# A two-layer transformer on one core: the first layer's attentions write their outputs by feature, their division moves into the stage that reads them

## The chip, the core and the metric

The kernel runs on one core of a Trainium2 chip. The core has TensorE (PE in the profile; its weight loads are listed as PEld), VectorE (DVE), ScalarE (ACT), GpSimd (POOL) and SyncE (SP), whose queue issues most transfers. Each engine works through its own instructions in order and waits at semaphores. The metric is the device time of one execution in microseconds, median over the runs shown. About 0.2% (some 7 us) is what a measurement of this kernel can tell from no change.

## What is computed

Batch 8, 512 tokens, 320 features, 20 heads of 16, a context of 64 tokens; two layers of self-attention, cross-attention and a gated feed-forward part. Only the first layer's attentions change; it is plain floating point:

```
def _attn(x, ctx, wq, wk, wv, wo, bo, heads):
    q = (x @ wq).reshape(b, n, heads, dh).transpose(0, 2, 1, 3)
    k = (ctx @ wk).reshape(b, j, heads, dh).transpose(0, 2, 1, 3)
    v = (ctx @ wv).reshape(b, j, heads, dh).transpose(0, 2, 1, 3)
    sim = jnp.einsum('bhid,bhjd->bhij', q, k) * scale
    a = jax.nn.softmax(sim, axis=-1)
    out = jnp.einsum('bhij,bhjd->bhid', a, v)
    out = out.transpose(0, 2, 1, 3).reshape(b, n, heads * dh)
    return out @ wo + bo
h1 = _ln(x, n1_g, n1_b)
x = _attn(h1, h1, q1, k1, v1, o1_w, o1_b, heads) + x
h2 = _ln(x, n2_g, n2_b)
x = _attn(h2, context, q2, k2, v2, o2_w, o2_b, heads) + x
h3 = _ln(x, n3_g, n3_b)
proj = h3 @ ff_w1 + ff_b1
a, g = jnp.split(proj, 2, axis=-1)
x = a * jax.nn.gelu(g, approximate=False) @ ff_w2 + ff_b2 + x
```

The second layer has the same shape, with operands rounded to 8 bits in its attentions, and does not change.

## The kernel before

**Stages.** `transformer` runs one stage after another; at the end of a stage all engines meet. In the first layer: `dense_phase` "qkv" (to 207 us of the trace), `self_attention` (207 to 699), `dense_phase` "q" (to 850), `cross_attention` (853 to 1028), `dense_phase` "ff" (to 1550). Attention results go from stage to stage through DRAM. A group of attention is 4 heads of one sample: 5 groups a sample, 40 in all.

**Self-attention.** A group is 8 units (`for j in range(UNITS)`). In unit j TensorE does, for the group two ahead, two score tiles `nat` [128 queries x 512 keys] (`natural`, L1250), whose row maxima VectorE reduces one tile at a time (L1391); then the transposed scores of its own group, `sT` (`transposed`, L1259), on which ScalarE takes the exponential into `probs` (L1325); then, for the group before, `products` (L1277). One call of `products` is 4 matmuls in fp32, which the profile counts as 8 instructions; a group has 8 calls. There are three `nat` banks, and tile t waits until the reduction of tile t-3 is done:

```
wait(pe, "a_nat_free", 16 * n + t - 2)
```

The maxima are split by GpSimd into three bf16 parts, turned on TensorE (`turn_shift`), copied and sent into the query stack as extra rows. Each output column block has 32 rows, 16 of the head's values and one of the exponentials' sum. `turn_output` (L1287) turns the result back to token order, ScalarE copies it twice (L1318, L1334), VectorE takes the reciprocal of the sums (L1385), GpSimd multiplies (L1352), SP stores 128 KB as rows of 256 bytes.

**Cross-attention.** The same with 64 keys, so that a group is one unit: `natural` for three groups ahead (L2017), `transposed` (L2026), `turn_shift` (L2034), `turn_output` (L2052), `products` (L2044). ScalarE: exponential, copy of the shift, two transfers of it (L2092), copy of the output (L2098). VectorE: two reductions (L2156), reciprocal (L2132), product (L2134). Meanwhile GpSimd splits weights of the coming stage (`loader.turn`, one job a group in the first eleven groups) and adds the output bias to the residual (`early.add`, L306, the first 32 groups).

**Dense stages.** `loop` walks the samples with a hand-written list of steps (`body`), several samples in flight. Here `oT` turns the attention output to feature order on TensorE (12 transposes a sample, L848), ScalarE rounds it (`oT_hi`, L949), VectorE subtracts (`oT_lo`, L1012), `oproj` multiplies by the output weights. The second layer's dense stages have `by_feature=True`: their input lies by feature already and `oT` needs no TensorE work.

## Time and profile before

| what | us |
|---|---|
| median of 3 runs | 3343.64 (3338.16 to 3344.39) |
| the profiled execution, its own time | 3342.7 |
| its span in the trace | 3341.0 |
| self-attention, one group in steady state | 11.57 |
| cross-attention, one group in steady state | 3.48 |
| feed-forward, one sample: first layer / second layer | 61.55 / 60.15 |
| "q" stage, one sample: first layer / second layer | 15.45 / 13.86 |

TensorE is busy 88% of the span, VectorE 65%, ScalarE 57%, GpSimd 24%. TensorE's granted clock is 0.84 on average and 1.00 inside the long stages. The periods in the table are differences between starts of the same operation: 39 of the copies L1318 for self-attention, the exponentials L2084 for cross-attention, the operations L804 (one a sample) for the dense stages. Busy times of TensorE overlap their neighbours' pipelines; starts tell more than durations there.

### The profile page before, as it was taken

The page shows a single profiled execution, that of the slowest core. Times are in us where ns is not written, and L with a number is a line of the kernel's source. Part 1 is how long each engine was busy: PE and PEld are TensorE (multiplying, and loading weights), DVE is VectorE, ACT ScalarE, POOL GpSimd, SP SyncE. Part 2 cuts the span into 40 slices and gives each one's busy share as a digit, 9 for nine tenths or more (in the row PEclk, how much of TensorE's full clock was granted, in tenths as well). Part 3 has the DMA queues.
Part 4 walks back from the last instruction along what each step waited for, and adds up shares of the span by engine and source line. Part 5 has one row for each costly group of instructions (what it writes and reads, how often), then busy time and mean ns, then how long its engine had stood idle before and what let it go on. Part 6 is the DMA issues. An engine that isn't in the chain of part 4 may idle for free. (4 is left out here: it accounts for less than half of the span.)

```text
span 3341.0 us, 47964 instructions
## 1 busy us (share of the span) xinstructions
PE 2936.9 (88%) x15594; PEld 1775.7 (53%) x15594; DVE 2157.7 (65%) x3834; ACT 1892.4 (57%) x3214; POOL 805.5 (24%) x1149
## 2 busy tenths in 40 slices
PE   6989999978696999998959999879978577899999
PEld 5754444457455888886731111111126342788888
DVE  5668888837453444444649999968868685444443
ACT  4328888844353232233549999989975355333322
POOL 2021221114640000000027888200003471200000
PEclk9969999989798999998975555555559898899999
DMA  8663333336762000001567557266723213010000
GB/s 228 211 166 101 106 107 103 90 80 158 165 176 46 10 10 19 9 0 38 152 173 163 128 137 164 32 90 83 97 56 96 79 45 92 26 36 18 25 17 16
DMA packets 358243, 296.57 MB, mean 89 GB/s; under 512 B 175602, under 2 KB 281914, under 8 KB 358058
## 3 DMA queue, kind: packets, MB, share of 16 engines
q1 hardware_dynamic: 347994, 273.93, 34.0%
q0 software_dynamic: 7280, 18.07, 2.1%
q10 hardware_dynamic: 2784, 2.29, 0.4%
q8 instruction: 94, 1.54, 0.2%
q14 instruction: 91, 0.75, 0.1%
HBM read 177.53 MB, written 114.52 MB: 87 GB/s over the span
## 5 line engine op out<-in xcount | busy, mean ns | idle before, releaser
L1591 PE MATMUL nat<-k_stack,q_stack 48*128 48x512 bf16 x640 | 381.0, 605 | 71.5 <-DMA k_stack<-k1w 31.1
L1391 DVE TENSOR_REDUCE neg_max<-nat 128x1 f32<-128x512 f32 x640 | 400.7, 682 | 61.3 <-PE nat L1250 61.2
L1625 DVE TENSOR_REDUCE m_all<-nat 128x1 f32<-128x512 f32 x640 | 423.3, 691 | 18.1 <-PE nat L1591 17.8
L804 POOL TENSOR_TENSOR rstd<-var_eps,neghalf 128x4 f32<-128x4 f32 x48 | 51.9, 1081 | 1588.0 <-DVE var_eps L1028 1588.0
L1645 ACT ACTIVATE nat<-nat,m_all 128x512 f32<-128x512 f32 x640 | 427.7, 2130 | 3.0 <-DVE m_all L1625 2.9
L1645 ACT ACTIVATION_READ_ACCUMULATOR nat<-nat,m_all 128x1 f32 x640 | 403.6, 1674 | 0.0
L1054 DVE SCALAR_TENSOR_TENSOR ff<-outp,bias,gel 128x512 f32<-128x512 f32 x160 | 120.1, 751 | 417.6 <-PE outp L326 417.6
L1325 ACT ACTIVATE probs<-sT 128x1024 f32<-128x1024 f32 x320 | 328.0, 1027 | 93.1 <-PE sT L1259 85.5
L968 ACT ACTIVATE gel<-outp,bias 128x512 f32<-128x512 f32 x160 | 110.0, 688 | 351.6 <-PE outp L326 351.6
L1839 ACT ACTIVATE exps<-sT 128x1024 f32<-128x1024 f32 x320 | 293.4, 1573 | 10.5 <-PE sT L1788 10.5
L972 ACT CAST ff_hi<-ff 128x512 fp32r<-128x512 f32 x160 | 99.2, 620 | 312.3 <-DVE ff L1054 312.3
L1591 PEld LDWEIGHTS nat<-k_stack,q_stack 48*128 48x128 bf16 x640 | 64.1, 102 | 387.9 <-ACT nat L1645 350.8
L1876 DVE TENSOR_SCALAR probs<-exps 128x1024 bf16<-128x1024 f32 x320 | 218.3, 692 | 67.8 <-ACT exps L1839 67.8
L1788 PE MATMUL sT<-q_stack,k_stack 51*128 51x512 bf16 x640 | 194.2, 604 | 34.6 <-DMA q_stack<-shift_rows 12.2
L1250 PE MATMUL nat<-k_stack,q_stack 48*128 48x512 f32 x640 | 200.8, 524 | 20.1 <-DMA k_stack<-k_hi 11.7
L1277 PE MATMUL o_ps<-probs,v_stack 128*32 128x256 f32 x2560 | 199.8, 394 | 1.1 <-issue 1.1
L1057 DVE TENSOR_TENSOR ff_lo<-ff,ff_hi 128x512 fp32r<-128x512 f32 x160 | 122.1, 763 | 109.7 <-ACT ff_hi L972 109.7
L1048 DVE TENSOR_TENSOR hT_lo<-h,hT_hi 128x512 fp32r<-128x512 f32 x144 | 111.6, 780 | 106.0 <-ACT hT_hi L963 105.7
L1250 PEld LDWEIGHTS nat<-k_stack,q_stack 48*128 48x128 f32 x640 | 80.0, 193 | 163.6 <-DVE neg_max L1391 129.2
L1259 PE MATMUL sT<-q_stack,k_stack 51*128 51x512 f32 x640 | 157.7, 430 | 0.5 <-ACT probs L1325 0.2
L1788 PEld LDWEIGHTS sT<-q_stack,k_stack 51*128 51x128 bf16 x640 | 34.0, 102 | 184.0 <-ACT exps L1839 165.7
L326 PE MATMUL outp<-hT_hi,Wff_hi 128*128 128x512 f32 x320 | 125.9, 393 | 4.6 <-DVE hT_lo L1048 4.6
(561 smaller groups left out, 7163.3 us busy)
## 6 DMA issues: line engine op xcount, KB each, us to landing
v<-vpad SPq DMA_DIRECT2D x64, 320.0 KB, 2.8
q_stack<-q_part SPq DMA_DIRECT2D x90, 160.0 KB, 5.8
k_stack<-k1w SPq DMA_DIRECT2D x90, 160.0 KB, 10.5
q_stack<-q_hi SPq DMA_DIRECT2D x160, 64.0 KB, 2.5
v_stack<-v SPq DMA_DIRECT2D x40, 256.0 KB, 3.2
q_stack<-q_hi SPq DMA_DIRECT2D x80, 128.0 KB, 2.8
raw<-v SPq DMA_DIRECT2D x16, 640.0 KB, 14.9
k_stack<-k_hi SPq DMA_DIRECT2D x158, 64.0 KB, 2.2
```

The source lines that it names most:

```text
L326: mm = pe.matmul(out, stay, move, start=(n == 0), stop=(n == len(terms) - 1))
L1250: pe.matmul(nat[(16 * n + t) % 3][:, :], q_stack[half, n % RING, pr, qt * P:(qt + 1) * P], k_stack[half, n % RING, pr, :], start=True, sto ...
L1259: mm = pe.matmul(sT[use % 2][:, ab, :], k_stack[half, n % RING, pr, kt * P:(kt + 1) * P], q_stack[half, n % RING, pr, :], start=True, stop ...
L1277: mm = pe.matmul(o_ps[VCOL * h:VCOL * h + VCOL, tok], v_stack[:, n % 2, kt, VCOL * h:VCOL * h + VCOL], probs[:, n % 2, h, kt, tok], start= ...
L1325: act.activation(probs[:, n % 2, 2 * pr:2 * pr + 2, kt, :], sT[use % 2][:, :, :], ACT.Exp, scale=DH ** -0.5).then_inc(s["a_turn_free"], 1)
L1391: dve.tensor_reduce(neg_max[:, n % 2, qt, 2 * pr + ab:2 * pr + ab + 1], nat[(16 * (n + 2) + t) % 3][:, :], AX.X, ALU.max, negate=True).the ...
L1591: pe.matmul(bank[i % NAT][:, :], q_stack[half, slot, g, pr, qt * P:(qt + 1) * P], k_stack[half, slot, g, pr, :], start=True, stop=True).th ...
L1625: dve.tensor_reduce(k.m_all[:, column(i // TILES, i % TILES)], bank[i % NAT][:, :], AX.X, ALU.max, negate=True).then_inc(s["e_max_ready"], 1)
L1645: act.activation(b[:, :], b[:, :], ACT.Exp, bias=k.m_all[:, col], accum_out=k.s_all[:, col]).then_inc(s["a_nat_free"], 1)
L1788: mm = pe.matmul(sT[u % TURNS][:, ab, :], k_stack[half, slot, g, pr, kt * P:(kt + 1) * P], q_stack[half, slot, g, pr, :], start=True, stop ...
L1839: act.activation(exps[:, u % EXPS], sT[u % TURNS][:, :, :], ACT.Exp).then_inc(s["a_turn_free"], 1)
L1876: dve.tensor_scalar(probs[:, u % KEPT], exps[:, u % EXPS], ROUND, -ROUND, ALU.add, ALU.add).then_inc(s["e_rounded"], 1)
```

## The change

Both first-layer attentions store the untransposed, undivided product tile (`o_sb`, 128 rows of 2 KB, 256 KB a group), two buffers in turn. Once a sample, the 20 rows of sums are read back from DRAM into an 80 x 128 tile (`load_sums`), VectorE takes one reciprocal (`invert`), and the shares are stored (`store_shares`); in self-attention GpSimd first splits them into a high and a low part (`split_shares`). The dense stage that follows loads the output by feature and multiplies it on VectorE (step `scale`): in "q" against a PSUM tile that one TensorE matmul with a 0/1 matrix `spread` makes from the 40 rows of shares, in "ff" against an SBUF tile that eight transfers fill by broadcasting. `oT` loses its transposes; the ff stage issues 8 loads a sample instead of 5.

In self-attention `turn_output`, its two copies' second, the per-group reciprocal and product go, and the 8 calls of `products` stand two by two in units 1, 3, 5 and 7. In cross-attention `turn_output` goes, VectorE instead of ScalarE copies the output, the query loads are issued for two groups at a time, the shift goes in one transfer, GpSimd does a loader job every fourth group (4 jobs instead of 10) and the bias in the last 32 groups; the other 6 jobs of `ff_w2` are done by GpSimd at the start of the ff stage, as in the second layer.

TensorE in self-attention, from the start of unit 1 to the start of unit 5. In the names nat_172 to nat_174 are the three score banks, sT_175 and sT_176 the two transposed ones. Before:

```order
L1250 MATMUL nat_172<-k_stack,q_stack 128x512
L1250 MATMUL nat_173<-k_stack,q_stack 128x512
L1259 MATMUL sT_175<-q_stack,k_stack 128x512 x2
L1267 MATMUL sT_176<-identb,parts 32x128 x4
L1277 MATMUL o_ps<-probs,v_stack 32x256 x4
L1250 MATMUL nat_174<-k_stack,q_stack 128x512
L1250 MATMUL nat_172<-k_stack,q_stack 128x512
L1259 MATMUL sT_175<-q_stack,k_stack 128x512 x2
L1287 MATMUL sT_176<-ident,o_sb 128x128 x4
L1277 MATMUL o_ps<-probs,v_stack 32x256 x4
L1250 MATMUL nat_173<-k_stack,q_stack 128x512
L1250 MATMUL nat_174<-k_stack,q_stack 128x512
```

Now:

```order
L1315 MATMUL nat_171<-k_stack,q_stack 128x512
L1315 MATMUL nat_172<-k_stack,q_stack 128x512
L1324 MATMUL sT_174<-q_stack,k_stack 128x512 x2
L1332 MATMUL sT_175<-identb,parts 32x128 x4
L1342 MATMUL o_ps<-probs,v_stack 32x256 x8
L1315 MATMUL nat_173<-k_stack,q_stack 128x512
L1315 MATMUL nat_171<-k_stack,q_stack 128x512
L1324 MATMUL sT_174<-q_stack,k_stack 128x512 x2
L1315 MATMUL nat_172<-k_stack,q_stack 128x512
L1315 MATMUL nat_173<-k_stack,q_stack 128x512
L1324 MATMUL sT_175<-q_stack,k_stack 128x512 x2
L1342 MATMUL o_ps<-probs,v_stack 32x256 x8
```

The output's transposes (L1287) and the single calls of products (x4) of units 2 and 3 are gone from here; unit 1 and unit 3 end with two calls (x8), unit 2 with none.

TensorE in cross-attention, one group. Before:

```order
L2017 MATMUL nat_246<-k_stack,q_stack 128x128 x4
L2017 MATMUL nat_247<-k_stack,q_stack 128x128 x4
L2026 MATMUL sT_248<-q_stack,k_stack 128x512 x2
L2034 MATMUL sT_249<-identb,parts 32x128 x4
L2052 MATMUL o_ps_250<-ident,o_sb 128x128 x4
L2044 MATMUL o_ps_251<-probs,v_stack 64x512 x2
```

Now:

```order
L2086 MATMUL nat_245<-k_stack,q_stack 128x128 x4
L2086 MATMUL nat_246<-k_stack,q_stack 128x128 x4
L2095 MATMUL sT_247<-q_stack,k_stack 128x512 x2
L2103 MATMUL sT_248<-identb,parts 32x128 x4
L2113 MATMUL o_ps_250<-probs,v_stack 64x512 x2
```

The four transposes L2052 between the turning of the shift and the products are gone.

VectorE in the "q" stage, the second half of a round, from the normalised rows z to the last addition of oproj; the next round follows with the statistics of x_resid. The banks oT hold the turned output before, and the spread shares now. Before:

```order
L1034 TENSOR_SCALAR z<-x_resid,mv,rstd 128x320 x4
L1016 TENSOR_TENSOR x_resid<-x_resid,oproj_224 128x320
L1048 TENSOR_TENSOR hT_lo<-h_214,hT_hi 128x512 x2
L1016 TENSOR_TENSOR x_resid<-x_resid,oproj_225 128x320
L1048 TENSOR_TENSOR hT_lo<-h_214,hT_hi 128x512
L1016 TENSOR_TENSOR x_resid<-x_resid,oproj_224 128x320
L1016 TENSOR_TENSOR x_resid<-x_resid,oproj_225 128x320
```

Now:

```order
L1092 TENSOR_SCALAR z<-x_resid,mv,rstd 128x320 x4
L1074 TENSOR_TENSOR x_resid<-x_resid,oproj_225 128x320
L1106 TENSOR_TENSOR hT_lo<-h_215,hT_hi 128x512 x2
L1074 TENSOR_TENSOR x_resid<-x_resid,oproj_226 128x320
L1106 TENSOR_TENSOR hT_lo<-h_215,hT_hi 128x512
L1064 TENSOR_TENSOR attn_T<-attn_T,oT_229 128x512
L1064 TENSOR_TENSOR attn_T<-attn_T,oT_230 128x512
L1074 TENSOR_TENSOR x_resid<-x_resid,oproj_225 128x320
L1064 TENSOR_TENSOR attn_T<-attn_T,oT_229 128x512
L1074 TENSOR_TENSOR x_resid<-x_resid,oproj_226 128x320
```

Three multiplications attn_T (L1064) have come in behind the last hT_lo, before and between the last two additions of oproj, and the differences oT_lo now read their result. The diff, cut to its core:

```diff
 dense_phase:
+        scale = [("scale", m) for m in range(3)] if recips is not None else []
-            between = [[("tail", 0)], oT[0:2], oT[2:], oproj[0:2], oproj[2:], [("stats", 0)], [("norm", 0)],
+            between = [[("tail", 0), *scale], oT[0:2], oT[2:], oproj[0:2], oproj[2:], [("stats", 0)], [("norm", 0)],
...
-                    zT[0], zT[1], oproj[1], zT[2], oproj[2], oproj[3]]
+                    zT[0], zT[1], oproj[1], zT[2], *scale[0:2], oproj[2], *scale[2:], oproj[3]]
...
+                        heads = rows(attn_in, b * (QUADS * P), QUADS * P).rearrange("(h c) t -> h c t", c=VCOL)[:, 0:DH, :]
+                        loads = [(attn, heads)]
...
+                        for tile, src in loads:
+                            for c in range(2):
+                                sp.dma_start(tile[:, c, :], src[8 * c:8 * c + 8]).then_inc(s["attn_in_loaded"], 16)
...
+                        pe.matmul(bank_of(st, r)[:, :], spread[:, m * P:(m + 1) * P], shares[:, :], start=True, stop=True
+                                  ).then_inc(s[turned[st][0] + "_full"], 1)
...
+                        dve.tensor_tensor(attn[:, m, :], attn[:, m, :], share, ALU.mult).then_inc(s[done], 1)
 self_attention:
+                    for r in range(2):
+                        wait(sp, f"a_o_stored{r}", 16 * ((QUADS * (b + 1) - r + 1) // 2))
+                    sums_of = rows(out, b * (QUADS * P), QUADS * P).rearrange("(h c) t -> h c t", c=VCOL)[:, DH, :]
+                    sp.dma_start(sums, sums_of.rearrange("h (x t) -> h x t", t=P)
...
-                def turn_output(n):
...
-                PRODUCTS = {1: (0,), 2: (1,), 3: (2,), 4: (3, 4), 5: (5,), 6: (6,), 7: (7,)}
+                PRODUCTS = {1: (0, 1), 3: (2, 3), 5: (4, 5), 7: (6, 7)}
...
-                        act.copy(o_sb[:, :], o_ps[:, :]).then_inc(s["a_o_copied"], 1)
+                        wait(act, f"a_o_stored{n % 2}", 16 * (n // 2 - 1))
+                        act.copy(o_sb[:, n % 2, :], o_ps[:, :]).then_inc(s["a_o_copied"], 1)
...
-                            act.copy(o_turned[:, n % 2, :], output_bank(n - 2)).then_inc(s["a_turn_free"], 1)
...
+                    pool.tensor_copy(share_hi, shares).then_inc(s["a_share_split"], 1)
...
+                    dve.reciprocal(shares, sums).then_inc(s["a_recip"], 1)
 cross_attention:
-                    for n in range(LOOK, RING):
-                        load_q(n)
+                for pair in range(2, PAIRS):
+                    load_q(pair)
...
-                        for pr in range(2):
-                            act.dma_start(words(q_stack[QROWS:ROWS, (n + 2) % RING, pr, :]),
+                        act.dma_start(words(q_stack[QROWS:ROWS, (n + 2) % RING, :, :]), words(shift_sb[0:12, n % 2, :])
...
-                    loader.turn(pool, n)
-                    if n < BATCH * TT:
-                        early.add(pool, n)
+                    if n % 4 == 3 and n // 4 <= len(loader.jobs):
+                        loader.turn(pool, n // 4)
+                    if n >= NQ - BATCH * TT:
+                        early.add(pool, n - (NQ - BATCH * TT))
...
+                    dve.tensor_copy(o_sb[:, n % 2, :], o_ps[n % 2][:, :]).then_inc(s["x_o_copied"], 1)
```

## Rows read from the trace of the kernel before

**Rows 1.** Busy time by engine in stretches (us, instructions), clock, DMA share, GB/s:

```profile
753.10:799.46 46.36, 40.64 (x240) 33.66 (x240) 36.86 (x79) 23.66 (x40) 20.68 (x28) 1.00 0.67 168
858.00:915.00 57.00, 44.52 (x218) 27.86 (x218) 21.71 (x40) 20.43 (x28) 45.86 (x97) 0.71 0.81 179
915.00:1015.00 100.00, 99.25 (x628) 57.80 (x626) 54.43 (x113) 56.26 (x86) 43.88 (x138) 1.00 0.62 159
940.00:980.00 40.00, 40.00 (x257) 23.59 (x256) 22.65 (x46) 22.61 (x35) 19.55 (x56) 1.00 0.70 178
1165.04:1411.23 246.19, 246.19 (x1346) 219.19 (x1345) 106.42 (x204) 74.29 (x116) 15.83 (x8) 1.00 0.06 13
3018.29:3258.88 240.59, 240.59 (x1296) 214.11 (x1296) 106.45 (x204) 74.72 (x116) 15.82 (x8) 1.00 0.07 21
```

**Rows 2.** TensorE's timeline in self-attention: start, us, operation, idle before it:

```profile
449.91 0.54 PE L1250 MATMUL nat<-k_stack,q_stack 48*128 48x512 f32 x2
...
451.26 0.49 PE L1250 MATMUL nat<-k_stack,q_stack 48*128 48x512 f32 x1 [0.21 <-DVE neg_max L1391]
...
453.65 0.63 PE L1287 MATMUL sT<-ident,o_sb 128*128 128x128 f32 x4
...
456.01 0.54 PE L1250 MATMUL nat<-k_stack,q_stack 48*128 48x512 f32 x2
...
456.72 1.07 PE L1277 MATMUL o_ps<-probs,v_stack 128*32 128x256 f32 x16
457.72 0.50 PE L1250 MATMUL nat<-k_stack,q_stack 48*128 48x512 f32 x2
...
458.38 0.64 PE L1277 MATMUL o_ps<-probs,v_stack 128*32 128x256 f32 x8
458.95 0.55 PE L1250 MATMUL nat<-k_stack,q_stack 48*128 48x512 f32 x2
```

**Rows 3.** VectorE's timeline in the same stretch:

```profile
458.26 3.80 DVE L1391 TENSOR_REDUCE neg_max<-nat 128x1 f32<-128x512 f32 x6 [0.42 <-PE nat L1250]
```

**Rows 4.** Timeline of one group of cross-attention:

```profile
942.75 1.38 ACTq L2092 DMA_DIRECT2D q_stack<-shift_sb  x2
...
943.05 1.11 PE L2017 MATMUL nat<-k_stack,q_stack 96*128 96x128 f32 x8
...
944.22 0.59 ACT L2098 COPY o_sb<-o_ps 128x512 f32<-128x512 f32 x1 [1.51 <-issue]
...
944.94 0.66 PE L2052 MATMUL o_ps<-ident,o_sb 128*128 128x128 f32 x4
...
945.52 1.08 PE L2044 MATMUL o_ps<-probs,v_stack 128*64 128x512 f32 x4
...
946.53 0.33 PE L2017 MATMUL nat<-k_stack,q_stack 96*128 96x128 f32 x1
```

**Rows 5.** Who waited for whom, start of cross-attention: us, times, longest:

```profile
PEld sT L2034 <- POOL parts L2119: 13.3, 8, 3.2
```

**Rows 6.** Groups of instructions: VectorE's, busy us and mean ns:

```profile
L1391 DVE TENSOR_REDUCE neg_max<-nat 128x1 f32<-128x512 f32 x640 | 400.7, 682 | 61.3 <-PE nat L1250 61.2
...
L2132 DVE RECIPROCAL recip<-o_ps 128x16 f32<-128x16 f32 x40 | 10.3, 258 | 45.4 <-PE o_ps L2052 27.8 <-DMA cross_out<-o_nat 17.6
...
L2541 DVE RECIPROCAL red<-red 128x1 f32<-128x1 f32 x1 | 0.2, 164 | 0.0
```

**Rows 7.** Timeline from cross-attention's end into the feed-forward stage:

```profile
1023.21 1.08 PE L2044 MATMUL o_ps<-probs,v_stack 128*64 128x512 f32 x4
...
1028.87 2.09 SPq L691 DMA_DIRECT2D attn_nat<-cross_out  x4
...
1039.56 0.60 PE L326 MATMUL misc<-q_hi,oT_hi 128*128 128x320 f32 x1 [1.49 <-DVE oT_lo L1012]
```

**Rows 8.** Transfer rate in 40 one-us slices of cross-attention:

```profile
GB/s 83 196 255 151 135 102 233 227 197 277 245 215 208 105 244 177 99 48 26 99 221 199 155 153 209 270 201 244 262 259 206 99 264 183 97 99 155 251 170 87
```

**Rows 9.** Transfer issues of cross-attention: count, KB each, median us to landing:

```profile
cross_out<-o_nat SPq DMA_DIRECT2D x40, 128.0 KB, 2.6
```

290 lines of the change are left out of this document (167 added, 123 removed).

## The prediction

> **What bounds the kernel now.** I read the busy time by stage first, then the timelines of one group. The averages hide that each stage has its own limit, and that only the six stages between 207 us and the end of the first feed-forward stage can move.
>
> Self-attention is TensorE and VectorE in turns. A pair of score tiles and a pair of transposed tiles each take about 0.33 us (the two matmuls of a pair run side by side): in unit 5 `nat` starts at 456.01 and the products at 456.72. Eight product instructions last 0.57 to the next `nat` (458.38 to 458.95), sixteen last 1.00 (456.72 to 457.72) [rows 2]. The only stall inside the group is at 451.26, where the second tile of unit 1 waits 0.21 us for a reduction, 1.35 us after unit 0's first tile went out at 449.91 [rows 2]. VectorE is not full either: in the same stretch it waits 0.42 us for TensorE, then does six reductions in 3.80 us [rows 3]. So neither is the bound; the three score banks couple them.
>
> Cross-attention is TensorE back to back in steady state (99.25 of 100 us), with the 16 DMA engines at 0.62 on average and 0.70 in the densest 40 us [rows 1]. One group there: score tiles at 943.05, output turned at 944.94, products at 945.52, next score tiles at 946.53 [rows 4]. Its first stretch is different: TensorE is busy 44.52 of 57 us at a granted clock of 0.71, GpSimd 45.86 [rows 1], and turning the shift waits 8 times, 13.3 us in all, for GpSimd's `parts` [rows 5].
>
> **Self-attention, per group.** The change takes TensorE's output turn away: 454.20 - 453.65 = 0.55 us [rows 2]. It also moves the products into the odd units, and that costs the banks. A reduction lasts 0.68 us [rows 6] and the next starts (3.80 - 0.68) / 5 = 0.62 after it [rows 3]; a tile's reduction can start when its matmul is over, 0.54 us after the tile (the length of the pair at 449.91) [rows 2]. So a bank is free some 0.54 + 0.68 + 0.06 = 1.28 us after its tile starts, 0.06 being my estimate for the two signals. The row measured 1.35 [rows 2], and I keep that for the upper end. Tile t waits for tile t-3, that is, the second tile of a unit waits for the first of the unit before. An even unit now has 0.66 us of work and no products behind it; the next unit's second tile starts 1.28 us after the even unit's first, then follow 0.33 + 0.32 until the products and 1.00 of products: 2.93 us for a pair of units. The pair with the shift's turn gets 0.17 more. The group: 3.10 + 3 x 2.93 = 11.89, against 11.57. This is +0.32 x 37 groups = +11.8. ScalarE, with one copy less, does not set this. The last groups have no score tiles for a later group; there the turn is pure gain, 2 x 0.55, and the drain behind the last product loses a copy and the division, which I estimate at 0.8: -1.9. **Self-attention +9.9.** Bounds: lag 1.35 gives 12.17 a group, so +0.60 x 37 - 1.9 = +20.3. Below, TensorE's own work is 8 x 0.66 + 4 x 1.00 + 0.33 = 9.6 us and the reductions' 16 x 0.62 = 9.9, which no order of three banks reaches.
>
> **The "q" stage.** Its head now waits for a chain behind the last output: store (2.6 us to landing [rows 9], as before), the sums' load back (no row; like the store, 2.6), the reciprocal, GpSimd's split, the shares' store, the loads, one matmul, three multiplications. The reciprocal of 128 columns: 16 take 258 ns and 1 takes 164 [rows 6], 6.3 ns a column, so 164 + 127 x 6.3 = 0.96 us. The split is two small GpSimd copies, 0.9 by estimate. What goes is the old turn, copy, reciprocal and product. Part of the chain runs beside the stage's start (weights, statistics). I take +2.0 for the head and +1.8 for the second sample's load, which is issued behind it: +3.8, between 1 and 8. In the rounds TensorE saves 12 transposes, four of which last 0.55 [rows 2], so some 1.6 us less one to three matmuls of 0.2, say 1.2; VectorE gets 3 multiplications of about 0.6 us at the end of the round, on the path to the next statistics. The stretch shows TensorE busy 40.64 of 46.36 us and VectorE 36.86 [rows 1], so neither covers the other: +0.3 a round, from -0.3 to +1.8, times 7: +2.0. The second layer's 13.86 a round has neither cost. **"q" +5.8.**
>
> **Cross-attention.** The output's turn leaves TensorE: 945.52 - 944.94 = 0.58 us a group [rows 4], 3.48 - 0.58 = 2.90. ScalarE loses its output copy of 0.59 and one of two transfer issues (1.38 for both) [rows 4], so it isn't the bound afterwards; VectorE exchanges reciprocal and product for one copy. I take 2.95, a little waiting: -0.53 x 31 = -16.4. In the first groups GpSimd's loader jobs go from every group to every fourth: the 13.3 us of waits [rows 5] go, -13.3. The bias, moved to the last 32 groups, is GpSimd work beside a mostly idle engine (43.88 of 100 [rows 1]). The first pair of query loads has to land whole, +1.7. **Cross-attention -28.**
>
> The stores grow from 128 to 256 KB a group [rows 9]. At 178 GB/s for a share of 0.70 [rows 1] the extra 128 KB are 0.74 us x 0.70 = 0.52 of share-time, on top of 0.70 x 3.48 = 2.44; over 2.95 us the share would be 1.00. That is too much for comfort, yet slices of 1 us reach 277 GB/s [rows 8], and in them the same kinds of rows move; 750 KB in 2.95 us are 254 GB/s. The densest stretch lasts only part of the stage; at the mean share, 0.62, it is (2.16 + 0.50) / 2.95 = 0.90.
>
> The new rows are 2 KB long, the old 256 bytes. The Trainium skill ("DMA: Bandwidth & Descriptors", Why small descriptors are slow) counts 256/32 + 3 = 11 cycles for a descriptor of 256 bytes; by that rule the new store would cost 2 x 67 / 88 = 1.52 times the old one, not twice, so half of the 0.52. No row here decides it, and the sum stands without it.
>
> **The "ff" stage.** A round loses the 12 transposes and comes to look like the second layer's: 246.19 / 4 = 61.55 against 240.59 / 4 = 60.15 us [rows 1]. Six rounds in steady state: -8.4. Its head: before, the first load is issued 5.66 us after the last products (1023.21, 1028.87), the first `oproj` matmul comes at 1039.56 [rows 7]. Now the store, the sums' load (2.6), the reciprocal (0.96) and the shares' store (2.6) come first, +6.2; gone are turn, reciprocal and product (about 1.5) and the transposes and their copies (1.7): +3.0, and 0.6 for more loads a sample. Six `ff_w2` jobs on GpSimd run beside the first rounds, where it is busy 15.83 of 246 us [rows 1]: nothing. **"ff" -4.8**, between -8 and +1.
>
> The second layer's code is the same: 0. **Sum:** +9.9 + 5.8 - 28 - 4.8 = -17.1 on the profiled execution's 3342.7; it lies 0.9 under the median, which gives 3326.5.
>
> **The rivals.**
>
> *Self-attention gains.* If the pairs of units overlapped better than the bank rule says, say at 10.7 a group, between 9.9 and 11.89, self-attention would give -0.87 x 37 - 1.9 = -34, and the time 3326.5 - 44 = 3282. For it: TensorE loses work. Against: the stall at 451.26 already shows the rule with products in the unit before it, and even units without products leave 0.62 us bare [rows 2].
>
> The Trainium skill ("TensorEngine Tiling (Array Packing)", PSUM Bottleneck) says that tiling speeds up TensorE but not the reading of PSUM. The idle row at 451.26 agrees: a tile waits for its reduction, so by that rule less TensorE work shows in the time only where the reductions keep up.
>
> *Cross-attention gains less.* If the DMA engines carry 0.92 of the denser stretch, a group takes 2.96 / 0.92 = 3.2 and the stage gives -8.7 for the period, -9 for the head: -18; with a lag of 1.30 to 1.31 self-attention costs 12.0 a group, +14, and "q" +7. Sum -1.8: 3342. For it: the transfers' share of 1.00 above. Against: rates of 277 GB/s.
>
> *The slower side: the DMA engines bound cross-attention.* The highest share that a long stretch shows is 0.81 [rows 1]. If that is what they carry, a group takes 2.96 / 0.81 = 3.65, longer than 3.48; it decides from a share-time of 2.8 a group on. The period costs +5 (0.17 x 31), the gain at the head goes into the same transfers, and the whole is +9.9 + 5.8 + 5 - 4.8 = +16: 3359. For it: at 0.81 GpSimd was the one who was late, so higher was never asked for. Against: exactly that reason, and [rows 8].
>
> *The change doesn't do what it says:* the order shows the turns gone in both stages, so I give it nothing.
>
> **How the numbers follow.** My forecast 0.60, self-attention gains 0.09, cross-attention gains less 0.20, the slower side 0.11. The forecast's own unknowns (self-attention +10 to +20, "q" +2 to +12, cross-attention -34 to -22, "ff" -8 to +1) spread it over some 3300 to 3344. The range leaves out the fast rival and the slow one: 3298 to 3347. A measurement of this kernel tells 0.2%, 6.7 us, from no change. Faster than 3337: 0.56 of the forecast, all of the 0.09 and 0.05 of the third, 0.70; slower than 3350: 0.11 and a little, 0.12; between: 0.18.
>
> **What would show it.** In the changed kernel a self-attention group of 11.9 us (12.2 with the longer lag, under 11.3 if I am wrong), VectorE idle before `neg_max` by TensorE four times a group, and TensorE idle 0.6 us by VectorE before the second tile of units 1, 3, 5 and 7. In cross-attention 2.95 us a group with TensorE unbroken, or 3.2 to 3.65 with waits on transfers of `q_stack`, and the waits for `parts` gone. "q" rounds of 15.7 us, and "ff" rounds of 60.2. The first `oproj` of "ff" some 19 us behind the last products instead of 16.4. A self-attention group at or under 11.57 would break the largest uncertain term; a cross-attention group above 3.3 would break the largest gain.

## The result

The changed kernel takes 3412.96 us (median of 4 runs, 3406.32 to 3429.98), the kernel before 3343.68: a ratio of 1.0219, with a 95% interval of 1.018 to 1.0258. It is slower by 69 us where 17 us less were forecast. The profiled execution took 3406.3 us with a span of 3404.4.

Where it went, by the start of the same operation in both traces (first reduction of self-attention; last `products`; the operation `rstd`, one a sample; first exponential of cross-attention; and so on), with what the prediction had for the stretch:

| stretch | before | after | change | forecast |
|---|---|---|---|---|
| self-attention | 487.6 | 499.1 | +11.5 | +9.9 |
| to the first `rstd` of "q" | 26.9 | 41.3 | +14.4 | +3.8 |
| the seven rounds of "q" | 107.4 | 148.4 | +41.0 | +2.0 |
| to the first exponential of cross-attention | 42.2 | 46.1 | +3.9 | +1.7 |
| cross-attention | 151.3 | 140.5 | -10.8 | -29.7 |
| to the first `rstd` of "ff" | 26.5 | 37.7 | +11.2 | +3.6 |
| "ff" from there | 504.2 | 495.0 | -9.2 | -8.4 |
| second layer | 1786.6 | 1788.7 | +2.1 | 0 |

The rows sum to 64.1 us; the two spans (3341.0 and 3404.4) are 63.4 apart, since the stretch before self-attention is 0.8 shorter; the medians are 69 apart. Here are busy times by stretch (columns as in [rows 1]): the last six rounds of "q", cross-attention, a part of it, and four rounds of "ff", in the changed kernel.

```profile
768.70:896.50 127.80, 100.76 (x429) 77.81 (x428) 87.40 (x172) 46.88 (x77) 43.76 (x55) 0.81 0.38 119
942.00:1080.00 138.00, 127.63 (x670) 68.37 (x668) 74.99 (x116) 57.37 (x77) 70.66 (x202) 0.87 0.80 196
1010.00:1025.00 15.00, 15.00 (x52) 7.63 (x51) 6.64 (x10) 4.44 (x6) 5.07 (x15) 0.50 0.97 214
1233.10:1473.90 240.80, 240.80 (x1298) 214.22 (x1297) 113.50 (x216) 74.80 (x116) 15.80 (x8) 1.00 0.08 26
```

"q" is what stands out: TensorE is busy 100.76 of 127.80 us at a granted clock of 0.81, where [rows 1] had 40.64 of 46.36 at 1.00. Cross-attention runs at a DMA share of 0.80 and a clock of 0.87, and has a stretch of 15 us entirely at the lower clock (0.50, that is 1.2 GHz). The "ff" rounds are the 60.2 us that were forecast (240.80 / 4).

Where an experiment below has no interval, it is one run, and its stages say more than its time. The four runs of the changed kernel lie 24 us apart, and traces in which the code of a stage is the same give 499.1 to 501.1 us for self-attention (nine traces), 148.4 to 150.6 for the rounds of "q" (eight), but 137.8 to 144.8 for cross-attention (seven).

The timeline of one round of "q", from the last use of `attn_T` to the next sample's cast (start, us, operation, idle before it):

```profile
816.23 0.93 DVE L1070 TENSOR_TENSOR oT_lo<-attn_T,oT_hi 128x512 fp32r<-128x512 f32 x1
...
817.35 0.34 SPq L692 DMA_DIRECT2D shares<-self_shares  x1
...
817.88 1.61 SPq L696 DMA_DIRECT2D attn_T<-self_out  x2
...
819.69 1.22 SPq L698 DMA_DIRECT2D attn_T<-self_out  x2
...
827.14 1.22 PE L887 MATMUL oT<-shares,spread 40*128 40x512 f32 x2 [3.92 <-DMA attn_T<-self_out]
827.97 1.28 DVE L1064 TENSOR_TENSOR attn_T<-attn_T,oT 128x512 f32<-128x512 f32 x2 [2.05 <-PE oT L887]
...
831.55 0.69 DVE L1064 TENSOR_TENSOR attn_T<-attn_T,oT 128x512 f32<-128x512 f32 x1
...
833.98 1.14 ACT L990 CAST oT_hi<-attn_T 128x512 fp32r<-128x512 f32 x2 [8.78 <-PE oproj L326]
```

There is one tile `attn_T`. Its last reader is the third `oT_lo`, which ends at 817.16. The next sample's loads are issued at 817.35, 817.88 and 819.69, and land at 827.1. TensorE, due for the `scale` step of the same round some 6 us after the first issue, waits 3.92 us for them. In TensorE's order the matmuls with `spread` stand in front of the last two `oproj`, so these wait too. VectorE's three multiplications end at 832.24, but the cast that follows starts only at 833.98: what released it was the last `oproj`, which reads the tile that the cast overwrites. Then comes `oT_lo` again, and the circle closes, through TensorE's order as much as through the multiplications. The waits of the stretch 768 to 882 say it in two lines (us, times, longest):

```profile
ACT oT_hi L990 <- PE oproj L326: 43.8, 5, 9.1
...
PE oT L887 <- DMA attn_T<-self_out: 20.1, 5, 4.3
```

In the kernel before the same circle had slack:

```profile
769.24 0.66 PE L848 MATMUL oT<-ident,attn_nat 128*128 128x128 f32 x4 [1.32 <-DVE oT_lo L1012]
...
770.08 3.01 SPq L691 DMA_DIRECT2D attn_nat<-self_out  x4
...
780.54 1.03 PE L848 MATMUL oT<-ident,attn_nat 128*128 128x128 f32 x8
```

The tile was free as soon as TensorE had turned it, the loads were issued from 770.08 and had landed by 777.9, and the next turn was due only at 780.54: 10.5 us after the first issue, with 2.7 to spare.

Self-attention, TensorE, one group of the changed kernel:

```profile
412.08 0.49 PE L1315 MATMUL nat<-k_stack,q_stack 48*128 48x512 f32 x1 [0.30 <-DVE neg_max L1443]
...
413.73 0.50 PE L1315 MATMUL nat<-k_stack,q_stack 48*128 48x512 f32 x2
...
414.31 0.40 PE L1315 MATMUL nat<-k_stack,q_stack 48*128 48x512 f32 x1
415.01 0.50 PE L1315 MATMUL nat<-k_stack,q_stack 48*128 48x512 f32 x1 [0.31 <-DVE neg_max L1443]
...
417.96 0.50 PE L1315 MATMUL nat<-k_stack,q_stack 48*128 48x512 f32 x1 [0.32 <-DVE neg_max L1443]
...
420.97 0.50 PE L1315 MATMUL nat<-k_stack,q_stack 48*128 48x512 f32 x1 [0.37 <-DVE neg_max L1443]
```

The second tile of units 1, 3, 5 and 7 waits 0.30 to 0.37 us of TensorE's idle time for a reduction: 412.08, 415.01, 417.96, 420.97 are 2.93, 2.95 and 3.01 apart. That is the picture forecast, beside the one stall of 0.21 in [rows 2]; the idle time itself is about half of the 0.6 us that the prediction named as its sign.

### The profile page after: what moved, and what is told of

It is laid out like the page before. It is cut to its first block and busy times, and to the rows that moved or that the text cites. A ratio compares the mean times of both kernels' runs of the same rounds, so it can differ in the third digit from the quotient of the medians.

```text
span 3404.4 us, 46635 instructions
## 1 busy us (share of the span) xinstructions
PE 2913.3 (86%) x15106; PEld 1779.3 (52%) x15106; DVE 2199.1 (65%) x3820; ACT 1862.2 (55%) x3134; POOL 789.3 (23%) x1125
## 5 line engine op out<-in xcount | busy, mean ns | idle before, releaser
L1680 DVE TENSOR_REDUCE m_all<-nat 128x1 f32<-128x512 f32 x640 | 423.9, 690 | 18.3 <-PE nat L1646 18.0
L1380 ACT ACTIVATE probs<-sT 128x1024 f32<-128x1024 f32 x320 | 326.8, 1025 | 116.3 <-PE sT L1324 114.2
L1315 PE MATMUL nat<-k_stack,q_stack 48*128 48x512 f32 x640 | 236.9, 497 | 59.8 <-DVE neg_max L1443 47.3
L1843 PE MATMUL sT<-q_stack,k_stack 51*128 51x512 bf16 x640 | 194.1, 604 | 33.5 <-DMA q_stack<-shift_rows 10.9
L1315 PEld LDWEIGHTS nat<-k_stack,q_stack 48*128 48x128 f32 x640 | 96.7, 192 | 206.6 <-DVE neg_max L1443 142.6
L1324 PE MATMUL sT<-q_stack,k_stack 51*128 51x512 f32 x640 | 186.9, 433 | 1.1 <-ACT probs L1380 1.1
L1342 PE MATMUL o_ps<-probs,v_stack 128*32 128x256 f32 x2560 | 174.0, 386 | 0.9 <-issue 0.9
L990 ACT CAST oT_hi<-attn_T 128x512 fp32r<-128x512 f32 x96 | 56.0, 618 | 148.7 <-PE oproj L326 82.4
## 6 DMA issues: line engine op xcount, KB each, us to landing
k_stack<-k1w SPq DMA_DIRECT2D x90, 160.0 KB, 10.5
```

What stands on the lines that cost most here:

```text
L1315: pe.matmul(nat[(16 * n + t) % 3][:, :], q_stack[half, n % RING, pr, qt * P:(qt + 1) * P], k_stack[half, n % RING, pr, :], start=True, sto ...
L1324: mm = pe.matmul(sT[use % 2][:, ab, :], k_stack[half, n % RING, pr, kt * P:(kt + 1) * P], q_stack[half, n % RING, pr, :], start=True, stop ...
L1342: mm = pe.matmul(o_ps[VCOL * h:VCOL * h + VCOL, tok], v_stack[:, n % 2, kt, VCOL * h:VCOL * h + VCOL], probs[:, n % 2, h, kt, tok], start= ...
L1380: act.activation(probs[:, n % 2, 2 * pr:2 * pr + 2, kt, :], sT[use % 2][:, :, :], ACT.Exp, scale=DH ** -0.5).then_inc(s["a_turn_free"], 1)
L1680: dve.tensor_reduce(k.m_all[:, column(i // TILES, i % TILES)], bank[i % NAT][:, :], AX.X, ALU.max, negate=True).then_inc(s["e_max_ready"], 1)
L1843: mm = pe.matmul(sT[u % TURNS][:, ab, :], k_stack[half, slot, g, pr, kt * P:(kt + 1) * P], q_stack[half, slot, g, pr, :], start=True, stop ...
```

## Experiments: the q stage

In the diffs `...` stands for lines left out, and most semaphore updates (`then_inc`) and counts are left out too.

**Two tiles** (a_two_tiles). `attn_T` and `shares` twice in "q", used in turn, on the changed kernel:

```diff
-            attn = sb("attn_T", [P, 3, TOK])
+            attns = [sb("attn_T", [P, 3, TOK]) for _ in range(tiles)]
...
-                        sp.wait_ge(s["oT_split"], at["oT_split"] + split_b * 3 + 3)
+                        sp.wait_ge(s["oT_split"], at["oT_split"] + (split_b + 1 - tiles) * 3 + 3)
```

> The changed kernel, with two tiles attn_T and two tiles of shares in the q stage, used in turn, so that a sample's load starts two splits (oT_lo) earlier. Theory (the load of the single tile attn_T, 9 to 10 us from first issue to landing, is exposed in each round because its old content is read until oT_lo and the scale step of the same round needs the new): q rounds fall from 22 us to 15.4 to 16.5, the granted clock there rises from 0.8 to about 1.0, the time falls by some 45 us. Rival 1 (the added work, three multiplications and three matmuls, sets the round): rounds stay at 20 us or more. Rival 2 (the added transfers fill the DMA engines): rounds stay above 18 with a higher DMA share.

Measured 3370.38 us, 42.6 less than the changed kernel's median (35.9 in the span). The stretch of the rounds:

```profile
741.70:858.20 116.50, 93.90 (x485) 73.48 (x486) 97.44 (x198) 52.91 (x86) 47.02 (x58) 0.97 0.44 135
```

The seven rounds take 116.5 us instead of 148.4, at a clock of 0.97. That is just above the 15.4 to 16.5 us a round of the theory (16.6 on average). In the middle of the stage a round is 17.2 us, against 15.45 before; the 1.75 us are near the 3 x 0.6 of the multiplications, which are probably the second, smaller cost: no run takes them out. The head is 34.0 us instead of 41.3.

**The same work later** (a_scale_late). `scale` at the front of its own round, one tile:

```diff
-                ahead["scale"] = 3
+                ahead["scale"] = 2
-            body = [("stats", 0), *oT[0:2], items[0], oT[2], ...
-                    zT[0], zT[1], oproj[1], zT[2], *scale[0:2], oproj[2], *scale[2:], oproj[3]]
+            body = [("stats", 0), *scale[0:2], *oT[0:2], items[0], *scale[2:], oT[2], ...
+                    zT[0], zT[1], oproj[1], zT[2], oproj[2], oproj[3]]
```

> The changed kernel with one tile attn_T as it is, but with the scale step of a sample moved from the second half of the round before to the front of its own round, ahead of its oT steps (two samples ahead instead of three). The work is the same, the load gets about half a round more. Theory (the load is exposed): rounds of 16.5 to 18.5 us, so 25 to 40 us less in all, since the multiplications now stand in a chain with the casts. Rival (the work sets the round): 21 us or more.

3378.65 us; rounds of 18.3 on average, and the clock back at 0.97. The place of the step alone, with the same work and one tile, gives 20.4 us of the 41 back.

**A load that reaches more DMA engines** (a_compact). The share of the engines during the first load of the changed kernel's "q" stage, and the rate, in 40 slices of 0.35 us from 713 to 727 us:

```profile
DMA  0000004400327125555545423224432100000000
GB/s 0 0 0 0 23 15 103 101 16 0 146 88 59 41 70 187 205 199 193 217 193 159 95 77 94 76 100 101 95 66 31 1 0 0 0 0 0 0 0 0
```

The share is 5 tenths at some 200 GB/s while the transfers of 8 heads run and 2 to 4 tenths at 76 to 101 GB/s while those of 4 heads run. So I packed the values in DRAM when self-attention stores them:

```diff
-                        sp.dma_start(rows(out, (n - 2) * P, P), o_sb[:, n % 2, :])
+                        for h in range(4):
+                            sp.dma_start(rows(out, (n - 2) * 64 + DH * h, DH), o_sb[VCOL * h:VCOL * h + DH, n % 2, :])
+                        sp.dma_start(rows(out, NQ * 64 + (n - 2) * 4, 4), o_sb[DH:P:VCOL, n % 2, :])
...
+                            sp.dma_start(tile[:, 0:2, :], src[0:2 * P].rearrange("(c p) t -> p c t", p=P))
```

> The changed kernel, in which self-attention stores the 4 x 16 rows of values next to each other in DRAM (four transfers of 32 KB) and the 4 rows of sums apart (8 KB), so that the q stage loads a sample with one transfer of 512 KB over 128 partitions and two of 64 KB instead of two of 8 heads x 16 rows and two of 4 heads x 16 rows. One tile attn_T, products as in the changed kernel. Theory (the transfers by head reach only as many DMA engines as they have heads: the rate is 200 GB/s in the first part and 100 in the second, a share of 0.5 and 0.25): the load falls from 8.9 to 9.8 us to 5 to 7 us from first issue to the first matmul that waits for it, the q rounds from 21.2 us to 17 to 19 us, the stage's head by some 8 us, the time by 25 to 40 us. Rival (the load is slow because it stands behind the stores and the weight loads): under 8 us in all.

3376.76 us. The head and two of the loads, in slices of 1.05 us from 698 to 740:

```profile
GB/s 18 89 216 70 23 0 0 0 0 0 76 49 77 9 63 63 8 39 0 0 24 62 129 345 322 33 1 0 0 0 0 6 123 371 326 2 0 0 0 0
```

The loads now run at 322 to 371 GB/s, and the rounds take 116.4 us, the same as with two tiles: either cure is enough for the exposed load, and what remains (9 us over the 107.4 before) lies in the round's own work, by size the multiplications. Both together gave no more in the rounds (below). But self-attention grew by 5.4 us: single groups took up to 13.1 us.

## Experiments: self-attention

**The old spread of the products, on the changed kernel** (a_old_products):

```diff
-                PRODUCTS = {1: (0, 1), 3: (2, 3), 5: (4, 5), 7: (6, 7)}
+                PRODUCTS = {1: (0,), 2: (1,), 3: (2,), 4: (3, 4), 5: (5,), 6: (6,), 7: (7,)}
```

> The changed kernel with the calls of products spread over the units of a self-attention group as in the kernel before (one each in units 1, 2, 3, 5, 6, 7, two in unit 4). Theory (three score banks: the second tile of a unit waits for the reduction of the first tile of the unit before, so a unit without products leaves TensorE idle): the group falls from 12.04 us to 10.9 to 11.2, and the time by 32 to 44 us. Rival (reductions or exponentials set the group, or the copies): the group stays within 0.2 us of 12.04.

3371.77 us, a group 10.94 us instead of 12.07 (self-attention 462.0 instead of 499.1 us). TensorE's timeline keeps one stall, in unit 1:

```profile
340.52 0.50 PE L1315 MATMUL nat<-k_stack,q_stack 48*128 48x512 f32 x1 [0.22 <-DVE neg_max L1443]
...
342.03 0.49 PE L1315 MATMUL nat<-k_stack,q_stack 48*128 48x512 f32 x2
...
343.36 0.49 PE L1315 MATMUL nat<-k_stack,q_stack 48*128 48x512 f32 x2
...
344.60 0.54 PE L1315 MATMUL nat<-k_stack,q_stack 48*128 48x512 f32 x2
```

Units follow each other 1.24 to 1.33 us apart, about the 1.28 that a bank needs, and none of these waits. So taking the turn away is worth 0.63 us a group, and grouping the products costs 1.13.

**The grouping alone, on the kernel before** (b_grouped), the same edit the other way:

> The kernel before with the products of a self-attention group in four pairs (units 1, 3, 5, 7), nothing else. Theory (bank rule): the even units get bare time, of which the output's turn in unit 2 fills one; the group goes from 11.57 to 12.0 to 12.2 us, about as long as in the changed kernel, and the time rises by 17 to 24 us. Rival (the turn costs its 0.55 us wherever it stands, grouping costs 1.0): 12.6 us a group, plus 40 us. Rival 2 (grouping costs nothing; what made the changed group long is another part of it): 11.57.

3370.77 us, 12.38 a group: between the two theories. Units 2 and 3:

```profile
341.39 0.50 PE L1250 MATMUL nat<-k_stack,q_stack 48*128 48x512 f32 x2
...
342.06 0.65 PE L1287 MATMUL sT<-ident,o_sb 128*128 128x128 f32 x4
342.65 0.52 PE L1250 MATMUL nat<-k_stack,q_stack 48*128 48x512 f32 x2
343.25 0.50 PE L1259 MATMUL sT<-q_stack,k_stack 51*128 51x512 f32 x2
```

The turn at 342.06 does fill the bare time of unit 2, but it takes one of the two `sT` banks: the transposed scores of unit 3 start 0.60 us after their score tiles instead of the 0.34 of unit 2. Of the 0.31 us by which this group is longer than the changed kernel's, most lies there. That the bank is what they wait for is read from the order of the uses, not tried.

## Experiments: cross-attention

**Fewer bytes by fewer rows** (x_small_store). Only the 17 rows a head that are read later:

```diff
-                        sp.dma_start(rows(out, (n - 2) * P, P), o_sb[:, n % 2, :])
+                        for h in range(4):
+                            sp.dma_start(rows(out, (n - 2) * P + VCOL * h, DH + 1),
+                                         o_sb[VCOL * h:VCOL * h + DH + 1, n % 2, :])
```

> The changed kernel, in which cross-attention stores only the 4 x 17 rows of each output tile that are read later (16 of values and the sum for each head), in four transfers, 136 KB instead of 256 KB a group. Theory (the DMA engines bound cross-attention in its dense stretches: share 0.93 to 0.97, 741 KB a group at 216 GB/s are 3.4 us): with some 620 KB a group the mean distance of exponentials falls from 3.56 us to 2.9 to 3.15 and cross-attention takes 15 to 25 us less. Rival (the loads of two groups at once delay the small transfers of the shift, whatever the stores are): the waits of sT for q_stack<-shift_sb stay above 10 us in all and the stage changes by under 6 us. Rival 2 (the number of transfers counts, not their bytes): slower than before the edit.

3546.79 us: 134 us more than the changed kernel's median, for 120 KB less a group. Cross-attention took 260.6 us. The rate in slices of 1 us:

```profile
GB/s 25 27 25 65 203 297 215 209 103 75 64 47 25 17 58 154 190 27 43 28 16 98 320 207 213 27 27 25 61 47 25 27 61 320 215 233 41 27 41 41
```

Between the query loads the rate sits at 25 to 27 GB/s. Of the three outcomes written down, the second rival (the number of transfers counts) had the sign right, but nothing of this size; the rate looked like one DMA engine carrying a whole transfer, and the next run tells the two apart.

**Four transfers of 32 rows, the same bytes as the one** (x_four32):

```diff
-                        sp.dma_start(rows(out, (n - 2) * P, P), o_sb[:, n % 2, :])
+                        for h in range(4):
+                            sp.dma_start(rows(out, (n - 2) * P + VCOL * h, VCOL),
+                                         o_sb[VCOL * h:VCOL * h + VCOL, n % 2, :])
```

> The changed kernel with cross-attention's store as four transfers of 32 whole rows (64 KB each), the same bytes as one of 128 rows. In x_small_store four transfers of 17 rows ran at 25 to 27 GB/s, a sixteenth of the highest rate. Theory (17 rows can't be divided among several DMA engines and one carries them all; 32 can): cross-attention within 10 us of the 140 of the changed kernel. Rival (four issues a group in place of one are what cost 120 us): 200 us or more.

3436.31 us, cross-attention 161.0 us: neither theory's number. Against 17 rows the stage is 100 us shorter, so the 17 rows are what cost most; but four transfers in place of one still cost it 20.5 us. Where they lie:

```profile
DVE m_all L2194 <- DMA m_all<-cross_out: 19.5, 7, 4.7
...
PE nat L2088 <- DVE neg_max L2214: 14.6, 4, 5.2
```

VectorE waits 19.5 us for the sums to come back from DRAM (9.1 in the changed kernel), its reductions stand behind that wait, and TensorE waits 14.6 us for these, which it never did in the changed kernel. SyncE meanwhile waited 20.5 us for VectorE's copies (48.6 in the changed kernel), so its queue was fuller but not full. Whether the three issues more delay the sums, or stores in four parts land later, isn't told apart.

**Five transfers, 136 KB** (x_compact): the packing of the q stage's experiment, in cross-attention and "ff".

> The changed kernel with the same packing of the output in cross-attention: five transfers, 136 KB a group instead of one of 256 KB, and the ff stage loads a sample's values with one transfer over 128 partitions and two over 64. Theory 1 (bytes bound cross-attention): mean distance of exponentials from 3.56 us to 3.1 to 3.2, the stage 12 to 18 us shorter; the head of ff 3 to 6 us shorter, since half of its loads is now quick. Theory 2 (the stretches at the lower clock and what starts them bound it): the stage within 6 us. Rival (SyncE's queue becomes the bound, five issues a group instead of one are some 1.5 us more): the stage is longer, the stores start late.

3432.92 us, cross-attention 167.8 us. The bytes fell by 120 KB a group and the stage grew, so bytes don't bound it. SyncE's issues add up to 137.8 us of the 164.9 between first and last exponential (71.0 of 138.8 in the changed kernel), as the rival with the queue has it; but VectorE's wait for the sums is as long as with four transfers (19.7 us), and what delays them is again not told apart. "ff" got no faster head (37.4), since its loads of the shares still go by head.

**Twice the bytes** (x_double_store): each tile stored a second time.

```diff
+                        for copy in range(2):
+                            sp.dma_start(rows(out, (copy * NQ + n - 2) * P, P), o_sb[:, n % 2, :])
```

> The changed kernel, in which cross-attention stores each output tile twice, the second time to a place that nobody reads: 256 KB and one issue a group more. x_four32 had three issues more and no bytes and took 20.5 us more, so one issue is worth some 7 us. Theory (bytes bound the stage, 741 KB a group at 216 GB/s): 1000 KB a group are 4.6 us, the stage goes from 140 us to 180 or more. Rival (SyncE's queue, the chain of the sums or the bursts bound it): 145 to 155 us.

3422.67 us, cross-attention 153.3 us. The stretch 930 to 1080:

```profile
930.00:1080.00 150.00, 130.99 (x640) 73.57 (x640) 72.21 (x111) 50.73 (x69) 66.42 (x196) 0.77 0.95 239
```

The engines carry 239 GB/s at a share of 0.95. The changed kernel's 196 at 0.80 was no limit of the stage: 10 MB more cost 12.8 us, under a third of what the theory of the bytes needs. For short stretches its engines were as full (0.97 from 1010 to 1025), so that a small transfer can be late there is not excluded.

**Query loads for one group at a time** (x_single_q):

```diff
-                def load_q(pair):
+                def load_q(n):
...
-                    if exists(n - 1) and exists(n - 1 + RING) and n % 2 == 0:
+                    if exists(n - 1) and exists(n - 1 + RING):
```

> The changed kernel, in which cross-attention's query loads are issued for one group at a time again, as in the kernel before (three of 128 KB instead of three of 256 KB for two), with 8 semaphores instead of 4; the bytes are the same. Theory (bytes bound the stage): no more than 5 us less or more. Rival (bursts of 768 KB delay the shift's transfer behind them): the waits of sT for q_stack<-shift_sb fall from 15 us to under 5, the stage takes 10 to 20 us less.

3402.21 us. The first exponential comes 5.6 us sooner; the stage is 2.5 us shorter, which is inside the 7 us of its spread and not the 10 to 20 of the rival. TensorE's weight loads of `sT` waited for the shift's transfer 12 times, 13.9 us in all, from 942 to 1083 in the changed kernel; now:

```profile
DVE m_all L2191 <- DMA m_all<-cross_out: 16.7, 7, 4.6
...
PEld sT L2094 <- DMA q_stack<-shift_sb: 4.4, 4, 1.8
```

So the bursts did delay that transfer (from issue to landing 4.6 us at the median in the changed kernel, 3.1 now). What the stage kept is the wait of VectorE for the sums (12.2 us of the 16.7 lie before the last products at 1076.7; its reductions stand behind it) and, behind its start, 31 us at the lower clock, as many as the changed kernel has.

**The sums later** (x_lazy_sums):

```diff
-                    if exists(n - 3) and (n - 3) % PER == PER - 1:
-                        load_sums((n - 3) // PER)
+                    for last in range(NQ - 1, -1, -PER):
+                        if n == min(last + 5, NQ + 2):
+                            load_sums(last // PER)
...
-                    if exists(n - 4) and (n - 4) % PER == PER - 1:
-                        invert((n - 4) // PER)
+                    if exists(n - 7) and (n - 7) % PER == PER - 1:
+                        invert((n - 7) // PER)
```

> The changed kernel, in which cross-attention reads a sample's sums back two groups later, inverts them three groups later and stores the shares three groups later, with one wait more on SyncE so that the tile isn't overwritten. VectorE waited 9.1 us in six times for the read-back and SyncE 8.8 us in four times for the store ahead of it. Theory (these waits, and what is queued behind them, cost the stage): 10 to 18 us less. Rival (bytes, or the bursts): within 4 us of 140.5.

3405.72 us, cross-attention 135.9 us: 4.5 less than the changed kernel's 140.5, just beyond what the rival allowed and far from 10 to 18. It lies 1.9 us below the shortest of the seven traces with the same code, so at most the sign rests on it; the combinations below repeat it, with 135.4 against 142.2 us.

**What a short wait sets off.** TensorE in the changed kernel, around 1005 us:

```profile
1000.54 1.11 PE L2086 MATMUL nat<-k_stack,q_stack 96*128 96x128 f32 x8
...
1003.42 1.11 PE L2086 MATMUL nat<-k_stack,q_stack 96*128 96x128 f32 x8
1005.77 0.74 PE L2095 MATMUL sT<-q_stack,k_stack 102*128 102x512 f32 x2 [1.23 <-DMA q_stack<-shift_sb]
...
1006.90 1.98 PE L2113 MATMUL o_ps<-probs,v_stack 128*64 128x512 f32 x4
1008.80 1.97 PE L2086 MATMUL nat<-k_stack,q_stack 96*128 96x128 f32 x8
...
1014.11 1.97 PE L2086 MATMUL nat<-k_stack,q_stack 96*128 96x128 f32 x8
```

At full clock a group takes 2.88 us (1000.54 to 1003.42). At 1005.77 TensorE has waited 1.23 us for the shift's transfer; from there on the same products last 1.98 instead of 1.08 us, and groups are 5.3 us apart (1008.80 to 1014.11) for four groups. The clock row above shows the 0.50; it lasted from 1006.6 to 1030.5. The clock's other fall in this stage, at 979.3, lasted 6.8 us, so one wait's price is not a rule. Over the stage: 39 distances of 2.90 are 113.1 us and were 138.8; six of them, drawn out by the lower clock (4.2 to 5.3 us), hold 12.3 of the 25.7 us of excess, waits for transfers the other 13.4. The kernel before ran without a break from its ninth group on.

## Experiments: what the cures are worth together

**Two tiles and the old spread** (combo), the edits of a_two_tiles and a_old_products:

> The changed kernel with two tiles attn_T in the q stage and with the products of self-attention spread as in the kernel before. If the two costs are independent, the time is 3406 - 36 - 35 = 3335 us, just at the edge of what can be told from the kernel before (0.3 % faster). If one of them hid behind the other, 3350 or more.

3334.8 us (10 runs, 3328 to 3342), ratio 0.9973 of the kernel before, interval 0.9962 to 0.9983. The two costs are independent: self-attention takes 462.6 us here and 462.1 with the spread alone, the seven rounds 116.3 and 116.5 with two tiles alone. That the time hits the 3335 to the microsecond is luck; the runs spread over 14.

**With the store of 17 rows** (combo_small):

> The same combination with cross-attention's store of 4 x 17 rows instead of 128. Theory (bytes bound cross-attention): another 12 to 20 us less, 3315 to 3323 us, 0.6 to 0.9 % faster than the kernel before. Rival (bursts): 3335 as without it.

3468.79 us, ratio 1.0372 (1.0355 to 1.039): 134 us more than combo, the same as without the two cures.

**With self-attention's output packed** (combo_compact):

> The combination of two tiles attn_T and the spread products, with self-attention's output packed as in a_compact. The load is hidden in the rounds already, so only the stage's head (two exposed loads, 2 to 3 us each) and the chain in front of it gain: 3335 - 6 to 10 = 3325 to 3329 us. If the rounds of 16.6 us are still bound by transfers rather than by the three multiplications of VectorE, they fall to 15.5 and 8 us more go.

3379.45 us, ratio 1.0116 (1.0077 to 1.0155), 45 us more than combo instead of 6 to 10 less. The q stage was as before; self-attention went from 462.6 to 510.8 us, single groups from 10.9 to as much as 15.45. SyncE's queue, one group:

```profile
413.42 1.90 SPq L1273 DMA_DIRECT2D q_stack<-q_hi  x4
415.37 1.70 SPq L1273 DMA_DIRECT2D q_stack<-q_lo  x2
417.11 2.76 SPq L1288 DMA_DIRECT2D q_stack<-shift_sb  x4
419.92 0.88 SPq L1273 DMA_DIRECT2D k_stack<-k_hi  x2
420.84 0.89 SPq L1273 DMA_DIRECT2D k_stack<-k_lo  x2
421.78 1.17 SPq L1273 DMA_DIRECT2D k_stack<-k_hi  x2
422.99 1.81 SPq L1323 DMA_DIRECT2D self_out<-o_sb  x4
424.84 0.55 SPq L1325 DMA_DIRECT2D self_out<-o_sb  x1
```

Issue follows issue without a gap, 11.4 us of them a group against 9.3 in combo; the five stores hold 2.4. At 12.07 us a group this queue had a little room (5.4 us in all were lost in a_compact), at 10.9 it has none: a cure that was almost free beside one bound is the new bound beside another. That the queue is the bound is read from this, not tried with the stores on another queue.

**With query loads for single groups** (combo_single), **and then with the sums later** (combo_single_lazy), each on combo:

> The combination of two tiles attn_T and spread products, with cross-attention's query loads for one group at a time. x_single_q took 8 us off between the end of the q stage and the end of cross-attention. If that holds in the combination: 3335 - 8 = 3327 us; if it was chance of one run, 3335.

3323.22 us, ratio 0.9937 (0.9916 to 0.9958): 11.6 us less than combo. 7.8 of them lie before the first exponential (39.4 us instead of 47.2), a stretch that took 45.7 to 49.0 us in all thirteen traces with loads for two groups.

> The same with the sums read back and inverted later. If the waits of the chain cost the stage: 3312 to 3320 us; if not, as combo_single.

3315.21 us, ratio 0.9915 (0.989 to 0.9939): 29 us faster than the kernel before, and 98 less than the changed kernel. Its interval and that of combo_single overlap, so the last 8 us are likely, not certain. This is the version to keep. Its cross-attention takes 135.4 us; SyncE's queue has room for the single loads there (98 us of issues in 136 us of x_single_q).

## Why the prediction was wrong

The forecast missed by 81 us in the rows of the table: 50 in the "q" stage, 19 in cross-attention, 8 in the head of "ff", the rest in small change.

**The q stage, +55 us instead of +6,** is the largest part. The step that failed is the sentence that in the rounds "TensorE saves 12 transposes" while "VectorE gets 3 multiplications": it costs the engines and leaves out the tile, so the rounds' load stands in the sum at nothing. The old operation copied the loaded tile out early, so that it was free for the next load; the new one multiplies in place, so the load can't start before the last `oT_lo`, and TensorE asks for the next sample some 6 us after the issue, where it asked 10.5 us after it before. The two tiles show it (-32 us in the rounds), the later place confirms it (-20). The lower clock is part of it: at 0.81 over 128 us the stage spent about 49 us at half the clock, against 7 with two tiles.

**The load's length** was the second half of that step. The sum gave the second sample's load 1.8 us and took the first one to be as quick as before; each takes 8.7 to 10.1 us from its first issue to the matmul that waits for it, because a transfer of 8 heads ran at 200 GB/s and one of 4 at 100. Two such loads, one after the other, are most of the head of "q" (+14.4 instead of +3.8; with the packed store it is +4.8). The same is the head of "ff" (+11.2 instead of +3.6, priced there as "0.6 for more loads"):

```profile
1090.51 1.29 SPq L696 DMA_DIRECT2D attn_T<-cross_out  x2
...
1093.02 1.25 SPq L696 DMA_DIRECT2D shares<-cross_shares  x2
...
1106.14 1.90 DVE L1064 TENSOR_TENSOR attn_T<-attn_T,shares 128x512 f32<-128x512 f32 x3 [16.40 <-DMA shares<-cross_shares]
```

15.6 us from the first issue to the first multiplication; before it was 5.6 to the first transpose. The eight transfers by head are 1.5 MB at 100 to 200 GB/s. The first `oproj` of "ff" came 27.5 us behind the last products, where the prediction's sign said 19.

**Self-attention was right,** in its size as well: +11.5 against +9.9. The pair of units is the 2.93 us that the bank rule gave. The group came to 12.03 instead of 11.89, and every fifth to 12.27, the 0.95 us reciprocal on VectorE once a sample, which the sum had left out for self-attention. The experiments also show what the size hides: the turn's removal is worth 0.63 us a group, and the grouping costs 1.13. The rule of the Trainium skill that I cited there ("TensorEngine Tiling (Array Packing)", PSUM Bottleneck) agrees with the four stalls a group.

**Cross-attention, -11 instead of -30** (-7 instead of -28 with the way to its first exponential). "I take 2.95, a little waiting" is right for a group that runs free (2.88 to 2.90, and the first eight took 28.3 us, where 41 were measured before), and wrong as a mean, 3.56. The prediction had two rivals with the DMA engines as the bound; one put the stage at -18, nearer than my sum, but their mechanism, a share of 0.92 or 0.81 as the bound of the stage, is refuted: the engines carried 239 GB/s at 0.95 when asked. What the sum lacked is that with TensorE back to back and the transfers close behind it waits of 1 to 2 us come up, and that behind such a wait the clock can fall too. Bursts of 768 KB delayed the shift's transfer, and VectorE waited for the sums' read-back; which wait starts which stretch isn't settled for the whole stage, and differs from run to run, so the cause is known here by its kinds and not by its shares.

As to the new store with rows of 2 KB, the single packets in the two traces of cross-attention tell something: one of 256 bytes took 18 ns before, one of 2 KB 87 ns at the median and 122 on average after, loads among them. 512 of the first against 128 of the second make the new store 1.2 to 1.7 times the old one's engine time, by this estimate, for twice the bytes. The rule of the Trainium skill ("DMA: Bandwidth & Descriptors", Why small descriptors are slow) gave 1.52, and the traces agree with it; it decided nothing, since the engines didn't bound the stage.

**"ff" and the second layer** came as forecast from "ff"'s first `rstd` on (-9.2 against -8.4; +2.1 against 0).

## What to carry to other kernels

When an operation starts to work in place on a loaded tile, draw the circle: last reader, issue, landing, first user; the slack that the old copy gave is a cost of the change, and it is cheaper to find in the code than in the trace. Cost a transfer by its shape before you cost it by its bytes, and count the issues on its queue against the period of the loop that it would have after the change, not before. And where TensorE is full, price a short wait by what the clock does behind it, too.

## What the runs showed of the hardware

- The outermost count of a transfer set its rate here: 8 heads of 16 rows some 200 GB/s at a share of 0.5, 4 heads some 100 at 2 to 4 tenths, 17 rows 25 to 27 GB/s, 128 or 64 rows up to 371. At some 25 GB/s each it fits one of the 16 DMA engines for each of the outermost parts, and one for all where 17 can't be divided. That is an inference from the rates; no run shows the engines one by one.
- A wait of 1.23 us of TensorE in a stage that was otherwise full was followed by 24 us at a clock of 0.50 (groups of 5.3 us instead of 2.9), in which TensorE was busy without a break; another fall in the same stage lasted 6.8 us.
- An issue on SyncE's queue took 0.50 us on average (most 0.42, those of the shift 0.64). At 18.6 issues a group (9.3 us) self-attention ran in 10.95 us, at 22.6 (11.4 us) in 12.4.
